# Loads on two queues with weights four rows to a partition, v(0) ahead of z(0), and attention steps one FFN unit later

## What is computed

```python
x = x + gated_delta(layernorm(x))     # attention part
x = x + ffn(layernorm(x))
# gated_delta: q, k = x Wq, x Wk (64 wide); v = x Wv (128 wide)
#   beta = sigmoid(x Wb + bb); delta = softplus(x Wd + bd)
#   S_t = beta_t * S_{t-1} + delta_t * k_t v_t^T;  o_t = q_t S_t;  return o Wo
# ffn: Wn = clip(round(w / (mean|w| + eps)), -1, 1)   (three weights, 1408 x 512)
#   hidden = sigmoid(x W1^T) * (x W2^T);  return hidden W3^T
```

## Time and profile before

| what | us |
|---|---|
| median of 3 runs | 328.5 (328.18 to 328.82) |
| the profiled execution | 328.81 |
| its span in the trace | 327.1 |
| TensorE busy | 319.8 |
| VectorE busy | 210.1 |
| ScalarE busy | 142.4 |
| GpSimd busy | 107.4 |

### The profile page before, as it was taken

How to read it: one execution, slowest core, us unless ns; L and a number is a source line. 1 busy time by engine, 2 the same in 40 slices (tenths; PEclk the granted TensorE clock), 3 DMA queues, 4 the chain that set the end, 5 groups by cost and what they waited for, 6 DMA issues and landing times.

```text
span 327.1 us, 5876 instructions
## 1 busy us (share of the span) xinstructions
PE 319.8 (98%) x2152; PEld 176.1 (54%) x2152; DVE 210.1 (64%) x474; ACT 142.4 (44%) x281; POOL 107.4 (33%) x339
## 2 busy tenths in 40 slices
PE   7999999999999999999999999999999999999996
PEld 5888779874445444445454444454544444444445
DVE  6789899899998767366688543666886312433311
ACT  3687896789855571323143260231431102232200
POOL 7298325599913016980030136500201100000000
PEclk9999999999999999999999999999999999999999
DMA  6999900647841625300003051000030720000011
GB/s 180 382 388 395 360 4 0 104 91 133 125 85 32 114 49 81 113 0 2 0 2 64 2 129 61 7 2 0 2 64 0 93 102 1 0 2 0 0 66 64
DMA packets 45805, 26.99 MB, mean 83 GB/s; under 512 B 37584, under 2 KB 38352, under 8 KB 45776
## 3 DMA queue, kind: packets, MB, share of 16 engines
q1 hardware_dynamic: 45456, 26.62, 31.0%
q10 hardware_dynamic: 320, 0.00, 0.0%
HBM read 13.89 MB, written 4.19 MB: 55 GB/s over the span
## 4 chain that ended last, share of the span: by engine, by line
PE 78%; DVE 10%; DMA 3%; SPq 3%; ACT 2%; issue 2%; DVEq 0%; ACTq 0%
PE ffn L1199 40%; PE ffn L1217 23%; PE lev L1120 4%; DMA x_sb<-in_L_attn_x_dram 3%; PE ffn L1044 3%; DVE w_nat L841 2%; DVE X L854 2%; SPq L282 2%; PE lev L1077 2%; PE pd L1054 2%; PE oc L1104 1%; DVE abs_part L821 1%; DVE w_nat L848 1%; DVE xnT L989 1%; DVE sc L881 1%
## 5 line engine op out<-in xcount | busy, mean ns | idle before, releaser
L1199 PE MATMUL ffn<-w_nat,w12T 128*128 128x512 f16 x704 | 155.4, 379 | 0.6 <-DVE xnT L989 0.6
L1199 PEld LDWEIGHTS ffn<-w_nat,w12T 128*128 128x128 f16 x704 | 67.8, 98 | 83.0 <-issue 3.7
L1217 PE MATMUL ffn<-w3T,w_nat 128*128 128x512 f16 (+1 forms) x374 | 76.7, 366 | 0.0
L718 ACT ACTIVATE xnT<-ffn 128x512 f32<-128x512 f32 x44 | 26.1, 593 | 97.5 <-PE ffn L1199 97.5
L989 DVE SCALAR_TENSOR_TENSOR xnT<-ffn,xnT 128x512 f32<-128x512 f32 x44 | 30.2, 687 | 52.3 <-PE ffn L1199 51.9
L1217 PEld LDWEIGHTS ffn<-w3T,w_nat 128*128 128x128 f16 x374 | 36.6, 98 | 40.7 <-ACT w_nat L724 1.0
L402 POOL TENSOR_TENSOR ve<-mv,rconst 128x2 f32<-128x2 f32 x12 | 2.5, 210 | 118.1 <-DVE mv L758 118.1
L1005 DVE SCALAR_TENSOR_TENSOR x_sb<-ffn,x_sb 128x512 f32<-128x512 f32 (+1 forms) x17 | 11.2, 659 | 42.8 <-PE ffn L1217 42.8
L994 DVE TENSOR_TENSOR w_nat<-xnT,w_nat 128x512 f16<-128x512 f32 x44 | 32.2, 732 | 0.4
L724 ACT ACTIVATE w_nat<-xnT 128x512 f16<-128x512 f32 x44 | 27.4, 623 | 8.4 <-DVE xnT L989 8.3
L881 DVE COPY_PREDICATED sc<-mask,lev 128x128 f32<-128x128 uint32 x56 | 18.9, 338 | 2.9 <-PE oc L1091 1.3
(11 more groups left out here) (142 smaller groups left out, 368.2 us busy)
## 6 DMA issues: line engine op xcount, KB each, us to landing
x_sb<-in_L_attn_x_dram SPq DMA_DIRECT2D x16, 256.0 KB, 8.4
out_dram<-x_sb SPq DMA_DIRECT2D x15, 256.0 KB, 2.0
w_nat<-in_L_ffn_w_dram SPq DMA_DIRECT2D x2, 1536.0 KB, 12.2
w_nat<-in_L_ffn_w_dram SPq DMA_DIRECT2D x2, 1408.0 KB, 14.7
w_nat<-in_L_ffn_w_dram SPq DMA_DIRECT2D x2, 1280.0 KB, 12.9
wv<-in_L_attn_Wv_dram SPq DMA_DIRECT2D x1, 256.0 KB, 5.8
wo<-in_L_attn_Wo_dram SPq DMA_DIRECT2D x1, 256.0 KB, 13.5
out_dram<-x_sb SPq DMA_DIRECT2D x2, 128.0 KB, 1.7
```

The lines of the kernel that those rows point to most:

```text
L718: nc.scalar.activation(sig[:, u % 2, :], bank[2 * u % 3][:, :], ACT.Sigmoid, scale=1.0 / XS).then_inc(sig_ready, 1)
L1199: done = nc.tensor.matmul(bank[n % 3][:, :], w12T[:, a * DT + t, u * P:(u + 1) * P], xT[:, g, part, t, :], start=t == 0 and part == 0, sto ...
L1217: done = nc.tensor.matmul(bank[(2 * HT + m + h) % 3][:, cols], hid[:, part, j, m * P:(m + 1) * P], w3T[:, j, cols], start=part == 0 and j ...
```

## The change

1. **Loads.** The projection weights are laid out four neighbouring rows to a partition (row 4p + t in place of row 128t + p); so that the product stays the same, the normalisations write `xn` with the columns in that order, which means that they read x with a step of four elements (`spaced`). Wq and Wk are issued by ACT's queue, behind the two loads of bb; the loads of bd move to SP. On SP Wv comes right behind x(0), then x(1), then Wb and Wd. x(4) goes ahead of the second half of the first FFN weight.
2. **Start of the projections.** v(0) of batch 0 is ahead of z(0) and the last six filler matmuls are gone. The transposes of chunk 1, batch 0, come between the two halves of z(0), batch 1 behind them, and ACT takes the first of their copies ahead of `zcopy(0)`.
3. **Dense stretch.** All attention steps stand one unit later (`fetch` stays); W3_AT is shifted to fit.

```diff
         w_in = [[sem(f"w{n + 1}_load{h}") for h in range(2)] for n in range(3)]
-        weights_in, wv_in, wo_in = sem("weights_in"), sem("wv_in"), sem("wo_in")
+        wqk_in, wbd_in, wv_in, wo_in = sem("wqk_in"), sem("wbd_in"), sem("wv_in"), sem("wo_in")
         bias_in = sem("bias_in")
...
+        def spaced(ap):
+
+            return ap.rearrange("p (n t) -> p t n", t=DT)
+
         def t_bank(c, b):
...
-        PE_AFTER = {"levels": (2, 7), "o": (4, 9), "wo": (5, 10)}
-        DVE_AFTER = {"chain0": (0, 5), "chain1": (0, 5), "masks": (2, 7), "state": (4, 9),
-                     "resid": (5, 11), "norm2": (5, 11), "apply": (6, 12), "xlo": (7, 12)}
...
+        PE_AFTER = {"levels": (3, 8), "o": (5, 10), "wo": (6, 11)}
+        DVE_AFTER = {"chain0": (1, 6), "chain1": (1, 6), "masks": (3, 8), "state": (5, 10),
+                     "resid": (6, 12), "norm2": (6, 12), "apply": (7, 13), "xlo": (8, 13)}
...
-        W3_AT = {4: (0, 1), 5: (2, 3), 6: (4,), 7: (5, 6), 8: (7, 8), 9: (9, 10)}
+        W3_AT = {4: (0, 1), 5: (2, 3), 6: (4, 5), 7: (6, 7), 8: (8, 9), 9: (10,)}
...
             load_x(0)
-            for dst, w in ((wqk[:, :, 0:K], Wq), (wqk[:, :, K:2 * K], Wk), (wbd[:, :, 0:K], Wb),
-                           (wbd[:, :, K:2 * K], Wd)):
-                sp_.dma_start(dst, w.rearrange("(t p) k -> p t k", p=P)).then_inc(weights_in, 16)
+            sp_.dma_start(wv[:, :, :], Wv.rearrange("(p t) k -> p t k", t=DT)).then_inc(wv_in, 16)
             load_x(1)
+            for dst, w in ((wbd[:, :, 0:K], Wb), (wbd[:, :, K:2 * K], Wd)):
+                sp_.dma_start(dst, w.rearrange("(p t) k -> p t k", t=DT)).then_inc(wbd_in, 16)
             load_x(2)
-            sp_.dma_start(wv[:, :, :], Wv.rearrange("(t p) k -> p t k", p=P)).then_inc(wv_in, 16)
             load_x(3)
+            for b in range(B):
+                sp_.dma_start(bias[half(b), 1:2], bd.rearrange("(k o) -> k o", o=1)).then_inc(bias_in, 16)
             load_w(0, 0)
+            load_x(4)
             load_w(0, 1)
-            load_x(4)
             load_w(1, 0)
...
                 nc.scalar.dma_start(bias[half(b), 0:1], bb.rearrange("(k o) -> k o", o=1)).then_inc(bias_in, 16)
-                nc.scalar.dma_start(bias[half(b), 1:2], bd.rearrange("(k o) -> k o", o=1)).then_inc(bias_in, 16)
+            for dst, w in ((wqk[:, :, 0:K], Wq), (wqk[:, :, K:2 * K], Wk)):
+                nc.scalar.dma_start(dst, w.rearrange("(p t) k -> p t k", t=DT)).then_inc(wqk_in, 16)
             nc.scalar.preload_act_table_set("natural_log_exp_and_others")
-            def evacuate_T(c):
+            def evacuate_first(c):
                 act.wait_ge(tile_T, 2 * c + 1)
                 if c > 1:
                     act.wait_ge(v_done, c - 1)
                 nc.scalar.activation(turned(c)[:, :, 0, :], tiles(t_bank(c, 0)[:, :]), ACT.Copy
                                      ).then_inc(xnT0_ready, 1)
+
+            def evacuate_T(c):
+                if c != 1:
+                    evacuate_first(c)
                 if c == C - 1:
...
                     act.wait_ge(tile_T, 2 * c - 3)
-                nc.scalar.activation(xn[:, c % 2, 0, :], tile(c, 0), ACT.Identity, scale=rs[:, c, 0:1],
+                nc.scalar.activation(tiles(xn[:, c % 2, 0, :]), spaced(tile(c, 0)), ACT.Identity, scale=rs[:, c, 0:1],
                                      bias=shift[:, c:c + 1]).then_inc(xn0_ready, 1)
...
             guess(1)
+            evacuate_first(1)
             zcopy(0)
...
                         dve.wait_ge(tile_T, 2 * c - 3 + b)
-                    nc.vector.tensor_scalar(xn[:, c % 2, b, :], tile(c, b), mv[:, c, b, 0:1], rs[:, c, b:b + 1],
-                                            ALU.subtract, ALU.mult).then_inc((xn0_ready, xn1_ready)[b], 1)
+                    nc.vector.tensor_scalar(tiles(xn[:, c % 2, b, :]), spaced(tile(c, b)), mv[:, c, b, 0:1],
+                                            rs[:, c, b:b + 1], ALU.subtract, ALU.mult).then_inc((xn0_ready, xn1_ready)[b], 1)
...
                     dve.wait_ge(tile_T, 2 * c - 2)
-                nc.vector.tensor_scalar(xn[:, c % 2, 1, :], tile(c, 1), mv[:, c, 1, 0:1], rs[:, c, 1:2],
-                                        ALU.subtract, ALU.mult).then_inc(xn1_ready, 1)
+                nc.vector.tensor_scalar(tiles(xn[:, c % 2, 1, :]), spaced(tile(c, 1)), mv[:, c, 1, 0:1],
+                                        rs[:, c, 1:2], ALU.subtract, ALU.mult).then_inc(xn1_ready, 1)
...
                 for a, w in enumerate((wqk, wbd)):
+                    if c == 0:
+                        pe.wait_ge((wqk_in, wbd_in)[a], 32)
+                        if a == 1:
+                            transposes(1, 0)
                     for t in range(DT):
...
             transposes(0, 1)
-            keep_warm(6)
-            pe.wait_ge(weights_in, 16 * 4)
+            pe.wait_ge(wv_in, 16)
+            pe.wait_ge(xnT0_ready, 1)
+            project_v(0, (0,))
             project_z(0)
-            pe.wait_ge(wv_in, 16)
-            project_v(0, (0,))
-            turn(1)
+            transposes(1, 1)
             project_v(0, (1,))
```

More of the change, by code:

```diff
@@ L236, in build_gated_delta_ternary_ffn @@
         LAST = (G - 1, DT - 1)
-        PE_AFTER = {"levels": (2, 7), "o": (4, 9), "wo": (5, 10)}
-        DVE_AFTER = {"chain0": (0, 5), "chain1": (0, 5), "masks": (2, 7), "state": (4, 9),
-                     "resid": (5, 11), "norm2": (5, 11), "apply": (6, 12), "xlo": (7, 12)}
-        ACT_AFTER = {"gt": (2, 7), "oT": (4, 9), "xhi": (7, 12)}
-        POOL_AFTER = {"fetch": (0, 3), "norm2": (6, 11), "xlo": (7, 12)}
+        PE_AFTER = {"levels": (3, 8), "o": (5, 10), "wo": (6, 11)}
+        DVE_AFTER = {"chain0": (1, 6), "chain1": (1, 6), "masks": (3, 8), "state": (5, 10),
+                     "resid": (6, 12), "norm2": (6, 12), "apply": (7, 13), "xlo": (8, 13)}
+        ACT_AFTER = {"gt": (3, 8), "oT": (5, 10), "xhi": (8, 13)}
+        POOL_AFTER = {"fetch": (0, 3), "norm2": (7, 12), "xlo": (8, 13)}
         W12_FRONT = 3
         W12_AT = {0: (3, 4), 1: (5, 6), 2: (7, 8), 3: (9, 10)}
-        W3_AT = {4: (0, 1), 5: (2, 3), 6: (4,), 7: (5, 6), 8: (7, 8), 9: (9, 10)}
+        W3_AT = {4: (0, 1), 5: (2, 3), 6: (4, 5), 7: (6, 7), 8: (8, 9), 9: (10,)}
         R12_AT = {0: (7,), 1: (8,)}
```

## The result

The changed kernel took 329.55 us (median of 21 executions, 329.15 to 333.14), the kernel before 328.54 us (21 executions, 327.79 to 329.42). The medians differ by 1.0 us (0.3%). The ratio of all executions is 1.0043, with a 95% interval of 1.0029 to 1.0057, which is 1.4 us, the difference of the means: slower, where 328.2 us and "no change" had been forecast. The profiled execution's span is 327.9 us against 327.1. What the two medians hide is the spread: three executions of the changed kernel took 330.5 to 330.7 us and two 333.1 us, while all 21 of the kernel before end by 329.4. In both of 333.1 us the mean granted clock of TensorE was 0.995 instead of 1.0.

The account below looks back on a forecast made before the run. The prediction took TensorE, busy for 98% of the span, as the bound. Terms: 328.81 + 0 - 1.1 + 0.7 + 0.1 = 328.5, less 0.31 gives 328.2 us; range 327.0 to 329.9.

Parts of the forecast that it names:

- Dense stretch, group 0 (-1.1): TensorE's waits for unit 3's product (0.55 us) and the state (0.49) both go: -1.1 us, between 0 and -1.4.
- The last W3 transpose (0 to 0.3, taken as 0): On SP's queue it stands behind chunk 2's two x transposes, ahead of the down projection: 0 to 0.3 us, taken as 0.
- Strided read (0.0): Eleven normalisations on VectorE and five on ScalarE read every fourth element: no change, 0.0 us.
- the strided read costs: Rival: strided normalisations slow the start and front; 330.2 us if each takes twice as long, 329.4 at half; chance 0.18.
- both rules weighed in the forecast: For the strided read: 16-byte lines want two accesses each for full bandwidth, against a step of four fp32 being free.
- Handovers (+0.8): Between groups, the last x transpose lands late for TensorE: 0.7 us at group 1, 0.1 at groups 2 to 3.
- the handovers keep up: Rival: the quick x transpose landing of 3.3 us holds at every handover, giving 327.3 us; chance 0.30.
- Start and first levels step (0.0): z(1) at 15.78 us, nothing gained; small gain at the first levels step cancels x(0)'s delay: 0.0, between -0.7 and +0.5.
- the rival with the half-priced strided read: The strided-read rival at half its price, +1.0 to +1.3 us in start and front: 329.4 us; rival's chance 0.18.

Follow-up runs that it names:

- the layout alone: The kernel before with only the four-rows-to-a-partition weight layout and the strided normalisation reads: 329.47 us, ratio 1.0029.
- The start alone: New loads, two queues and TensorE's new start, added to kernels with the layout: 329.88 against 329.47 us (old tables), 328.44 against 328.36 us (new tables, transpose moved).

## Why the prediction was wrong

**Dense stretch, group 0 (-1.1).** Right: both waits went, and -1.38 us lies at the end of the bounds (0 to -1.4).

**The last W3 transpose (0 to 0.3, taken as 0).** This is the step that failed, and the one that cost most: 1.18 us in the profile and 1.1 us in time. The forecast saw that it stands behind two x transposes and named their issue (1.3 us each), but put neither that nor the landing into a sum, and did not ask how much the transpose had to spare. In the kernel before it landed 0.4 us before TensorE wanted it. The forecast's own gain (the two waits) and wo(3), moved behind the first quarter of the down projection, bring TensorE there 2.1 us earlier; behind the x pair the transpose is issued only 0.7 us earlier. With the pair issued in 2.6 us, as forecast, 111.69 + 2.6 + 3.4 = 117.7 for a wish at 117.50 would have been a wait of some 0.2 us (an estimate), inside the bound; the pair took 3.38 us, for a reason that stays open, and the wait to TensorE's next matmul was 1.18. That moving this one transpose ahead of the pair takes the cost away is shown by two pairs of runs: 329.55 to 328.44 and 329.47 to 327.64 us.

**Strided read (0.0).** The second failed step. The rival "the strided read costs" named the right mechanism and one right place (ScalarE ahead of wo(1)); the price is 0.18 us on VectorE, below the 0.3 us from which it was to decide the sign, but 0.52 us on ScalarE, and ScalarE is the engine that TensorE waits for. The forecast took the bound from VectorE's rows alone, held the start to be the dear place and did not see the wait ahead of z(7); the layout alone shows nothing lost at the start (first levels step at 29.40 against 29.38) and all of its 0.84 us behind it. The Trainium skill (SBUF — State Buffer, section "Door 1: The DMA port swizzle") gives both rules weighed in the forecast; the rows side with the first (a line of 16 bytes wants two accesses), since a step of four fp32 was not free on either engine (1.32 against 0.80 us, 0.76 against 0.58).

**Handovers (+0.8).** Wrong by 0.8: no wait at any of the three. The pair was issued in 2.61 us, not 3.42, and landed in 3.2 us, not in 4.1 or 4.8, at 132.33 + 1.3 + 3.2 = 136.8 for TensorE at 137.23. One reading of the earlier trace rows was off as well: in the kernel before the second of the pair starts 1.3 us behind the first (128.09, not 128.9) and takes 2.14 us to issue, so with the landing of 4.1 us the spare time was 4.3 us, not 3.5. The rival "the handovers keep up" holds, and at the first handover the reserve is as small as the forecast worked out with the quick landing.

**Start and first levels step (0.0).** Nearly right. z(1) came at 16.18, not 15.78, with 0.98 us of idle time ahead, as foreseen; the wait for the chain fell to 0.30 us, below the 0.5 to 0.7 given, because TensorE comes later, not because VectorE is much earlier (29.32 against 29.38). The start alone costs 0.1 to 0.4 us.

**The sum.** With the measured terms: +0.79 (front, start and strided read together) - 1.38 + 1.18 + 0 = +0.6 us, and +0.8 by the spans. The forecast had 0 - 1.1 + 0 + 0.8 = -0.3. Two of its errors, the handovers (-0.8) and the strided read (+0.8), cancel, which is luck; what is left is the W3 transpose, less the 0.3 us that group 0 won beyond the forecast. That 329.55 us lies near the 329.4 of the rival with the half-priced strided read is luck too: that sum has its loss at the start, where there was none, and nothing for the W3 transpose.

## What to carry to other kernels

When an instruction moves behind others on a DMA queue, add up when they can start, their issue and its own landing, and set the sum against the moment at which it is wanted; look first how much it had to spare, because a gain elsewhere uses that up. Price a changed access pattern on each engine that runs it, and first on the one that the bottleneck waits for. When an edit in one place does nothing, look in the trace for the later wait that took its gain before giving up the theory.
